# A Mamba block and a mixture of experts on one core: router products, one dt product and half of an input projection go behind the spread of du, the output product is split over two steps, the norms of the routing branch come later

## What is computed

```python
xn = layernorm(x)
x1 = layernorm(xn) * ln_g + ln_b
def mamba(x1):                         # once forward, once on the reversed sequence
    xi, z = split(x1 @ in_w.T)         # 256 channels each
    xi = silu(causal_conv4(xi) + conv_b)
    dt, Bm, Cm = split(xi @ x_w.T)     # 8, 16, 16 columns
    delta = softplus(dt @ dt_w.T + dt_b)
    h[t] = exp(delta[t] * A) * h[t-1] + (delta[t] * xi[t]) * Bm[t]     # 256 x 16 states
    y[t] = sum_n h[t] * Cm[t] + xi[t] * D
    return (y * silu(z)) @ out_w.T
attn = concat(mamba(x1), reversed mamba) @ combine_w.T + combine_b + xn
e = argmax(xn @ router_w.T)            # 8 experts, one for each token
ffn = (silu(xn @ gate_w[e].T) * (xn @ up_w[e].T)) @ down_w[e].T
out = x + attn + ffn
```

## Time and profile before

| | |
|---|---|
| median of 3 runs | 923.8 us (922.23 to 923.9) |
| span of the profiled execution | 921.1 us |
| busy: DVE | 882.0 us, 96% |
| busy: POOL | 801.1 us, 87% |
| busy: PE | 736.6 us, 80% |
| busy: ACT | 699.8 us, 76% |

### The profile page before, as it was taken

How to read it: one execution, slowest core, us unless ns; L and a number is a source line. 1 busy time by engine, 2 the same in 40 slices (tenths; PEclk the granted TensorE clock), 3 DMA queues, 4 the chain that set the end, 5 groups by cost and what they waited for, 6 DMA issues and landing times. The chain is left out here.

```text
span 921.1 us, 10735 instructions
## 1 busy us (share of the span) xinstructions
PE 736.6 (80%) x3033; PEld 327.7 (36%) x3033; DVE 882.0 (96%) x631; ACT 699.8 (76%) x1183; POOL 801.1 (87%) x450
## 2 busy tenths in 40 slices
PE   8678877777488978979788987979786987878377
PEld 5233322231134534444343534436332431323022
DVE  5899999999899999999999999999999999999986
ACT  5798876646569789888989889998979776585531
POOL 1578786999999989998799898999798989999994
PEclk9978789788698999999999999989999799879578
DMA  7875342343265546445365636455554345553300
GB/s 229 224 221 144 109 111 58 139 100 101 110 162 158 152 154 175 138 136 149 134 151 177 156 84 209 124 185 125 181 140 134 85 95 163 108 170 75 85 0 12
DMA packets 87227, 123.45 MB, mean 134 GB/s; under 512 B 7929, under 2 KB 58490, under 8 KB 83202
## 3 DMA queue, kind: packets, MB, share of 16 engines
q1 hardware_dynamic: 85122, 118.58, 46.5%
q0 software_dynamic: 2048, 4.20, 1.5%
HBM read 75.44 MB, written 14.29 MB: 97 GB/s over the span
## 5 line engine op out<-in xcount | busy, mean ns | idle before, releaser
L1360 POOL TENSOR_TENSOR hs<-hs,C_rep 128x1024 f32<-128x1024 f32 x250 | 585.5, 2362 | 52.1 <-DVE hs L1150 27.8
L947 ACT ACTIVATE dA<-delta_rep,A_sb 128x511 f32<-128x511 f32 x512 | 338.2, 717 | 92.8 <-DVE hs L1150 47.1
L1131 DVE TENSOR_TENSOR in_b<-in_b,B_rep 128x1024 f32<-128x1024 f32 x256 | 300.1, 1216 | 15.7 <-PE in_b L589 14.7
L1150 DVE TENSOR_TENSOR_SCAN hs<-dA,in_b 128x1024 f32<-128x1024 f32 x128 | 285.3, 2267 | 5.3 <-PE y L623 5.3
L1148 DVE TENSOR_TENSOR_SCAN hs<-dA,in_b 128x1024 f32<-128x1024 f32 x128 | 285.1, 2267 | 1.4 <-PE y L623 1.4
L589 PE MATMUL in_b<-du,cst 128*128 128x512 f32 x256 | 160.8, 714 | 57.3 <-DVE hs L1150 43.6
L623 PE MATMUL y<-hs,cst 128*32 128x512 f32 x1024 | 139.5, 652 | 21.9 <-POOL hs L1360 21.9
L550 PE MATMUL front<-xpad,w_in 128*128 128x512 f32 x248 | 119.3, 616 | 9.0 <-ACT xi L876 7.3
L956 ACT ACT_TABLE_LOAD x71 | 91.1, 1283 | 8.3 <-PE moe L733 3.7
L589 PEld LDWEIGHTS in_b<-du,cst 128*128 128x128 f32 x256 | 46.8, 214 | 134.4 <-issue 132.6
L623 PEld LDWEIGHTS y<-hs,cst 128*32 128x32 f32 x1024 | 29.6, 116 | 113.8 <-issue 71.0
(11 more groups left out here) (147 smaller groups left out, 803.0 us busy)
## 6 DMA issues: line engine op xcount, KB each, us to landing
delta_rep<-tmpA SPq DMA_DIRECT2D x126, 256.0 KB, 3.9
C_rep<-dbc_scratch SPq DMA_DIRECT2D x16, 1024.0 KB, 7.2
B_rep<-dbc_scratch SPq DMA_DIRECT2D x15, 1024.0 KB, 5.0
gu_w<-in_gate_up SPq DMA_DIRECT2D x39, 384.0 KB, 3.8
dn_w<-in_down SPq DMA_DIRECT2D x39, 192.0 KB, 2.6
xs<-sorted_tokens SPq DMA_DIRECT2D x39, 64.0 KB, 3.9
sorted_ffn<-ys SPq DMA_DIRECT2D x39, 64.0 KB, 2.4
sorted_tokens<-up_f SPq DMA_DIRECT2D x9, 256.0 KB, 4.5
```

The costliest lines, as they stand in the source:

```text
L947: i = e.activation(dA[:, m % NA, r * L + 1:(r + 1) * L], src, ACT.Exp, scale=A_sb[:, d, 2 * p + jj, RH * rh + r:RH * rh + r + 1])
L1131: e.tensor_tensor(to, in_b[:, 2 + 2 * odd, :].unsqueeze(1).broadcast_to([P, RH, L]), by, ALU.mult).then_inc(dve_mult, 1)
L1150: e.tensor_tensor_scan(to[:, ::-1], a[:, 1:n + 1][:, ::-1], b[:, ::-1], 0.0, ALU.mult, ALU.add).then_inc(dve_scan, 1)
L1360: e.tensor_tensor(hs[:, m % NH, :], hs[:, m % NH, :], C_rep[:, u % 2, RH * rh:RH * rh + RH, :].rearrange("p r t -> p (r t)"), ALU.mult).th ...
```

## The change

- `ln_step` is 3c+1 plus the part's offset: sequence 0's, 1's, 2's and 3's pieces come one step later than before, sequence 4's stay, and those of 5, 6 and 7 come one step later. R0 goes from 27 to 28, and F0 stays at 56, since its distance is one less.
- PE: `router(c)` goes to the odd step of the pair of steps in which its part falls, where it stands behind the spread; `spread_du(0, 1)` stands ahead of the first skip product and of all of unit 1's input projection; the second half of unit 1's input projection stands behind `spread_du(0, 2)`; `dt_proj(v, 1)` of the odd units from 3 on is one step later, behind that step's spread; the first two of the four calls of `out_mm` are at step 11 instead of 12 for the first seven sequences.
- ACT: in a step, the copies of the first z products, of the logits and of the routing's inputs stand behind the step's decays instead of ahead of them.

```diff
 def ln_step(c, part):
-    return (0, 3, 6, 9, 13, 15, 18, 21)[c] + (-3, 0, 2, 3, 3, 4, 5)[part]
+    return 3 * c + 1 + (-3, 0, 2, 3, 3, 4, 5)[part]
...
+def routers(m):
+
+    return [c for c in range(NB) if ln_step(c, 5) // 2 * 2 + 1 == m]
...
 R0 = ln_step(NB - 1, 6) + 1
-F0 = R0 + 29
+F0 = R0 + 28
...
     if b < NB - 1:
-        return s0 + NSTEP + (12, 12, 12, 12, 10, 13, 13, 12)[k]
+        return s0 + NSTEP + (11, 11, 12, 12, 10, 13, 13, 12)[k]
...
             first_pair(1)
+            spread_du(0, 1)
             first_skip()
...
                 for v in fronts(m, -14, -14):
-                    in_proj(v, 1, 0)
+                    if v > 1:
+                        in_proj(v, 1, 0)
                 for v in fronts(m, -13, -13):
-                    in_proj(v, 1, 1)
+                    if v > 1:
+                        in_proj(v, 1, 1)
...
-                if m % 2 and m + 1 < LAST:
+                if m % 2 and m > 1 and m + 1 < LAST:
                     v, k = divmod(m + 1, NSTEP)
                     spread_du(v, k // 2)
+                for v in fronts(m, -13, -13):
+                    if v == 1:
+                        in_proj(v, 1, 0)
+                        in_proj(v, 1, 1)
...
-                for v in fronts(m, -9, -10):
+                for v in fronts(m, -9, -9):
                     dt_proj(v, 1)
-                for c in norms(m, 5):
+                for c in routers(m):
                     router(c)
...
             for m in range(STEPS):
-                if m == 0:
-                    keep_z(0, 0)
-                    keep_z(0, 1)
...
-                for c in norms(m, 6):
-                    keep_logits(c)
-                if m == R0 - 1:
...
                 if m + LEAD < LAST:
                     table(EXP_SET)
                     decay(m + LEAD)
+                if m == 0:
+                    keep_z(0, 0)
+                    keep_z(0, 1)
+                for c in norms(m, 6):
+                    keep_logits(c)
+                if m == R0 - 1:
...
```

More of the change, by code:

```diff
@@ L1055, in scalar_program @@
                     decay(m + LEAD)
+                if m == 0:
[4 more added lines that the diff above has]
+                if m == R0 - 1:
+                    e.wait_ge(act_logits, NB)
+                    e.copy(M[:, 0:256], logits[:, :, :].rearrange("p k e -> p (k e)")).then_inc(act_route, 1)
+                    e.copy(M[:, 256:512].rearrange("p (k e) -> p k e", e=E),
+                           cst[:, C_IOTA:C_IOTA + E].unsqueeze(1).broadcast_to([P, NBLK, E])).then_inc(act_route, 1)
                 for c in norms(m, 1):
```

## The result

The changed kernel has a median of 936.5 us (930.58 to 939.09, five runs); the kernel before has 923.9 over five runs beside it. The ratio is 1.0111, 95% interval 1.0086 to 1.0137. The forecast had the side right (slower) and the size wrong: 928.6 was 4.8 us more, measured were 10 to 13, and the range ended at 932.5. The changed kernel's single executions differ by almost 1%, so it matters which one was profiled: it is the fastest of the five (930.58, span 928.5), 7.4 us over the span of the kernel before.

The account below looks back on a forecast made before the run. DVE, 96% busy with scans, was taken to set the time, so only its idle time could change. 8.9 - 1.34 - 0.81 - 2.0 + 0 = +4.8 on 923.8 gave 928.6 us; range 920.0 to 932.5.

Parts of the forecast that it names:

- Spread of pair 1 early, pair 3: Unit 0: the waits of 3.41 us at pair 1 and 0.48 at pair 3 go, 3.9 us won.
- Pair 4: Unit 0: its multiply starts at 56.5 after a new wait of 4.5 us; of the 3.9 won nothing is left.
- The second store: Sequence 1's xn store, behind two broadcast loads, lands at 65.4; ACT stands some 7 us, pair 5 is 8.9 us later.
- faster rival: ACT's norm of sequence 2: store not in the way, pair 5 only 1.0 later; change -3.1, 920.7 us; chance 0.27.
- The rival that the store overtakes the broadcasts: Sequence 1's store lands 4.1 us after issue, at 61.3; pair 5 +4.8, in sum +0.7, 924.5 us; chance 0.13.
- Given back behind it: After pair 5, waits of 1.34 us at pair 6 and 0.81 in unit 1 go; both credited in full.
- more is lost: Step 18: sequence 5's store behind a delta load costs ACT 2.4 to 4.1 us more; 932.4 us; chance 0.10.
- dt product: Odd units, dt product behind the spread: waits of 0.66 and 1.34 us go, 2.0 won; lower end 0.
- smaller ones: The rest of DVE's 14.7 us of waits for spreads, beyond the waits named singly; no size given.
- Output product, copies: Output product in two steps on PE and copies behind ACT's decays: 0 each; product's bounds 1.83 us won or lost.

Follow-up runs that it names:

- again: The changed kernel run once more, unchanged: 935.0 us, ratio 1.0093 to the kernel before.
- store_first: The changed kernel with each store of xn ahead of the store of dbc and the broadcast loads in SP's queue: 923.7 us, ratio 0.9988.
- act_queue: The changed kernel, but ACT's own queue issues the store of sequence 1, behind the first dt output: 929.3 us, ratio 1.0046.
- clear_later: The changed kernel with the clearing stores from step 14 on instead of step 3: 934.9 us, ratio 1.0091.
- queue_only: The kernel before with only the store of sequence 1 issued one step later, behind unit 1's two broadcast loads: 935.0 us, ratio 1.0109.
- norms_only: The kernel before with the new `ln_step` alone, F0 kept: 939.2 us, ratio 1.0155.
- norms_ahead: The kernel before with the new `ln_step` and the store of xn ahead of the store of dbc in each step: 928.3 us, ratio 1.0028.
- clear_only: The kernel before with the clearing stores from step 14 on, nothing else: 926.5 us, ratio 0.9999.
- spread_only: The kernel before with pair 1's spread early and the second half of unit 1's projection behind pair 2's spread: 925.8 us, ratio 1.0006.
- dt_only: The kernel before with the second dt product of the odd units from 3 on behind the spread: 921.8 us, ratio 0.9965.
- dt_again: `dt_only` once more, on another chip: 921.9 us, ratio 0.9971.
- dt_clear: The kernel before with the odd units' second dt product behind the spread and the clearing stores from step 14 on: 917.0 us, ratio 0.9914.
- dt_clear2: `dt_clear` once more, on another chip: 918.1 us, ratio 0.9911.

## Why the prediction failed, by its own steps

**Spread of pair 1 early, pair 3: right.** Both waits are gone, and pairs 1, 2 and 3 follow each other at 6.6 us.

**Pair 4: right in kind, short by 2.2 us in one profile and exact in the other.** The start-up's 1.66 us aside, pair 4's multiply was forecast at 56.5 and came at 58.6. The dbc copy came where it was forecast (55.51 - 1.66 = 53.9, against 53.6). Behind it I took 1.12 us for the dt product and the spread "about as long"; here both took 2.07, at a granted clock of 0.50, after TensorE had idled 7.46 us ahead of the router product. In `again` it had idled 7.27 us and the x product took 3.52, but dt product and spread took 1.12 each:

```profile
54.79 1.12 PE L587 MATMUL front<-tmpB,w_dt 8*128 8x512 f32 x2 [0.67 <-ACT tmpB L910]
55.84 1.12 PE L594 MATMUL in_b<-du,cst 128*128 128x512 f32 x2
```

The granted clock from 54 to 58 was 0.50 in the first profile and 1.00 in `again`, where pair 4 came at 57.00 - 0.46 (its later start) = 56.5. `store_first`, `act_queue` and `clear_later`, with the same order up to here, are like the first profile.

**The second store: right in place and size.** The store was forecast to land 9.5 us after B_rep's issue; ACT went on 9.3 us after it (67.21 - 57.88, and the same in `again`). The 1.7 us taken off for two clearing stores that are gone from between fit. Pair 5 was forecast 8.9 us later; it is 10.67 with the start-up's 1.66, so 9.0, and in `again` 9.42 with 0.46, so 9.0 too. In the time, `queue_only` prices this place at 1.09%, 10 us (interval 8.0 to 12.2), where the forecast had 7.9 (8.9 less the 1.0 of its faster rival). What "the order of the queue" adds to the 2 MB themselves stays open: in the profile of `act_queue` the stall is as long on another queue, while half of the time came back. The rival that the store overtakes the broadcasts is dead: it did so on neither queue, though on ACT's it was issued a little ahead of C_rep's. The Trainium skill's rule, page "DMA: Bandwidth & Descriptors", section "Queues, rings and completion order", allows a later write to finish first; no run here shows that for a store behind two broadcasts. The same section says that the increment of the semaphore, which is what ACT waits for, lands only after every earlier write of that DMA engine, on all its queues; so the forecast read the rule too much in favour of this rival. That alone is not the whole of `act_queue`'s case, where the store's own packets ran until the microsecond from 66 to 67.

**"Given back behind it ... I take all", and the store of step 18 priced at nothing: this step failed.** I took 1.34 (pair 6) and 0.81 (unit 1, "since router and norm no longer stand ahead"). In unit 1, ACT stood 5.05 and 5.03 us for the store of sequence 5, and DVE waited 2.35 us (first profile) and 3.70 (`again`) behind that, where the kernel before has 1.27 and the forecast had left 0.5. The other kernels with the new norms and the store of sequence 5 behind the load have as much there: `act_queue` 3.86, `clear_later` 3.53, `norms_only` 4.49; with the stores ahead, `store_first` and `norms_ahead` have 0. No run moves the store of sequence 5 alone, so its price in the time is not measured by itself. I had seen this place: the rival "more is lost" names the store of sequence 5 behind the load of delta and says 2.4 to 4.1 us more on ACT. But I held it for unlikely, and its sum, 928.6 + 2.0 + 1.8, has no term for that wait.

Pair 6's wait is gone in the first profile; in the second it is 0.77, and a scan behind it waits 2.70 for the sum of states:

```profile
79.97 2.36 DVE L1143 TENSOR_TENSOR in_b<-in_b,B_rep 128x1024 f32<-128x1024 f32 x2 [0.77 <-PE in_b L594]
...
87.22 2.29 DVE L1160 TENSOR_TENSOR_SCAN hs<-dA,in_b 128x1024 f32<-128x1024 f32 x1 [2.70 <-PE y L628]
```

Windows of both profiles of the changed kernel (busy by engine PE, PEld, DVE, ACT, POOL; then the granted clock), `again` first:

```profile
70.00:80.00 10.00, 8.81 (x19) 4.05 (x18) 6.75 (x5) 7.38 (x16) 7.18 (x5) 0.50 0.58 136
80.00:90.00 10.00, 8.30 (x42) 3.77 (x46) 7.30 (x5) 8.19 (x18) 7.53 (x5) 0.60 0.41 105
```

and the first profile:

```profile
70.00:80.00 10.00, 8.35 (x20) 3.77 (x20) 6.27 (x4) 9.04 (x19) 5.77 (x4) 0.67 0.66 156
80.00:90.00 10.00, 8.55 (x51) 3.77 (x52) 9.93 (x8) 9.53 (x21) 9.92 (x6) 0.82 0.46 120
```

The sum of states took 3.64 us in `again` and 2.48 in the first:

```profile
83.51 3.64 PE L628 MATMUL y<-hs,cst 128*32 128x512 f32 x16
```

Over four profiles the scan's wait goes with that duration: 0 at 2.48, 0.40 at 2.71 (`act_queue`), 1.88 and 2.70 at 3.64 (`clear_later`, `again`). So the lower granted clock is the likely cause of this wait. But the stall for the store is not needed for it: `store_first` has no such stall, TensorE was busy for 9.33, 7.89 and 7.87 of each 10 us from 50 to 80 at a granted clock of 0.50, and the same 0.77 and 2.69 follow:

```profile
82.78 2.29 DVE L1160 TENSOR_TENSOR_SCAN hs<-dA,in_b 128x1024 f32<-128x1024 f32 x1 [2.69 <-PE y L628]
```

and `queue_only`, with the longest stall (10.13 us), has no wait for a sum in unit 0. Nor does this clock reach unit 1's waits: from 90 to 110 the granted clock was 1.00 in both profiles, and it fell to 0.60 and 0.50 (120 to 130) only after TensorE had been busy for 6.1 of 10 us, behind ACT's second stall. I made no run that holds the clock.

**dt product: right in place.** I took 2.0 for waits near 608 and 716. Both are there in every profile without this edit and gone in every profile with it. Measured alone it is 3.2 us (0.35%), and 2.0 lies within the interval. A third wait, of 3.35 us at 878.65 in the kernel before, the second longest of all, was counted among the "smaller ones" and is 0.64 in the changed kernel. It is 0.64 or 0.65 in `clear_only`, `spread_only` and `norms_ahead` too, which leave the dt product where it was, so this part of the last column isn't the product's.

**Output product, copies: right**, 0 for the first by measurement; the copies were not tried by themselves. I had said that near 308 a wait would stay; it did, 0.97.

**The norms beyond the store.** No term stood for them; `norms_ahead` measures 0.28%, 2.6 us.

**Against the times:** in fractions of the time before, the store's place is +1.1%, the norms +0.3%, the dt product -0.35%, others 0; that gives 1.0%, between the two measured ratios. The forecast had +0.5%. In us, as an estimate from these runs: the store's place 10.1 against 7.9, the spreads and what was "given back" 0 (`spread_only`, within its interval) against 1.0 - 1.34 - 0.81 = -1.15, the norms 2.6 against none, the dt product -3.2 against -2.0: 9.5 against 4.8. Also, the forecast stood against a profiled execution with 9.8 us of waiting up to pair 0, where the others shown have 10.3 to 11.2; by that difference, a single execution carries some 1 us of luck, which the range did not include.

## What to carry to other kernels

When steps move, list each engine's transfers in their new order, and ask of every small store that someone waits for what is now issued ahead of it: a large transfer, or a load that itself waits. An earlier issue cured both cases here; another queue gave back half of the loss, for reasons that are open. If a rival names a wait, put the wait into its sum. Do not credit the waits behind a long stall as healed; take them as bounds. And try the slow duration for all products behind an idle stretch, not only the first: four of five profiles here had it, the fifth did not.

## What I had not expected of the hardware

A 256 KB store issued on ACT's queue, where no other transfer ran in that stretch, took 9.1 us beside two 1 MB broadcasts that SP issued 0.4 us before and 0.2 us after it; the next one, on SP's queue without broadcasts, landed in 2.5 us. Leaving out three stores of 256 KB that SP issues behind its store changed nothing (`clear_later`: 8.1 us from issue to ACT's start with and without them). Two profiles of one kernel, with the same products behind the same idle stretch (7.46 and 7.27 us), had a granted clock of 0.50 and of 1.00 from 54 to 58 us. And two edits that measured 0.9999 and 0.9965 or 0.9971 alone gave 0.9914 and 0.9911 together (`clear_only`, `dt_only`, `dt_again`, `dt_clear`, `dt_clear2`).
